# A unit's convolution two slots behind its correlation products instead of one, with five x buffers, two volume buffers and an unrolled program

## The reference

```python
def _L0_conv_ref(feature, conv_w, conv_b):
    norm = jnp.sqrt(jnp.sum(feature * feature, axis=1, keepdims=True))
    fn = feature / jnp.maximum(norm, EPS)
    fp = jnp.pad(fn, ((0, 0), (0, 0), (PAD, PAD), (PAD, PAD)))      # PAD = 2
    sims = []
    for cc in range(5):
        for r in range(5):
            sims.append(jnp.sum(fp[:, :, r:h + r, cc:w + cc] * fn, axis=1))
    x = jnp.concatenate([feature, jnp.stack(sims, axis=1)], axis=1)  # 512 + 25 channels
    out = jnp.einsum('bihw,oi->bohw', x, conv_w) + conv_b[None, :, None, None]
    return jax.nn.relu(out)

x = x + _L0_conv_ref(_gn(x), L0_conv_conv_w, L0_conv_conv_b)   # _gn: 32 groups
x = x + _L1_conv_ref(_gn(x), L1_conv_conv_w, L1_conv_conv_b)   # the same form
```

## Time and profile before

| | |
|---|---|
| median of three runs | 577.4 us |
| span of the profiled execution | 584.5 us |
| PE busy | 510.0 us (87%) |
| DVE busy | 407.1 us (70%) |
| ACT busy | 259.9 us (44%) |
| POOL busy | 137.2 us (23%) |
| DMA queue share | 35.2% of 16 engines |

### The profile page before, as it was taken

The page is one execution under the profiler, slowest core; times in us unless marked ns, Lnnn a source line. Parts: engine busy times, 40 slices in busy tenths (PEclk is TensorE's granted clock), DMA queues, the critical chain, the costliest instruction groups (busy, mean ns, idle before and its releaser), DMA issues.

```text
span 584.5 us, 8565 instructions
## 1 busy us (share of the span) xinstructions
PE 510.0 (87%) x2888; PEld 287.5 (49%) x2888; DVE 407.1 (70%) x856; ACT 259.9 (44%) x350; POOL 137.2 (23%) x87
## 2 busy tenths in 40 slices
PE   0358779998999699997999979998999989998996
PEld 0246336464645446463464635555464646454442
DVE  5879697785868487756868477785978868672322
ACT  1343364635445263643645344453636364543332
POOL 3352625031030404012040400304040312204050
PEclk9986999999999989997999979999999999999999
DMA  8753103121135612355042721347132512334313
GB/s 342 255 192 134 57 4 102 38 88 56 52 115 164 207 38 88 127 177 181 14 128 113 226 91 34 118 167 230 32 100 85 202 38 70 110 119 140 128 41 144
DMA packets 47484, 69.37 MB, mean 119 GB/s; under 512 B 3848, under 2 KB 36616, under 8 KB 47448
## 3 DMA queue, kind: packets, MB, share of 16 engines
q1 hardware_dynamic: 47448, 68.93, 35.2%
HBM read 33.21 MB, written 35.71 MB: 118 GB/s over the span
## 4 chain that ended last, share of the span: by engine, by line
PE 45%; DVE 19%; issue 19%; POOL 8%; ACT 4%; DMA 3%; DVEq 1%; SPq 0%; ACTq 0%; POOLq 0%
PE conv_ps L456 32%; PE gram_ps L481 7%; DVE xs L806 3%; PE conv_ps L463 3%; DVE stats L639 3%; POOL corr L398 2%; POOL corr L396 2%; POOL mirror L393 2%; PE turn_ps L508 2%; DVE v L692 2%; ACT act_out L608 2%; DVE vol L703 2%; DVE opnd L697 2%; ACT vol L558 1%; DVE nbr L734 1%
## 5 line engine op out<-in xcount | busy, mean ns | idle before, releaser
L456 PE MATMUL conv_ps<-opnd,wh 128*128 128x512 f16 x512 | 198.4, 387 | 0.2 <-ACT act_out L608 0.2
L456 PE MATMUL conv_ps<-opnd,wl 128*128 128x512 f16 x512 | 198.3, 387 | 0.0
L456 PE MATMUL conv_ps<-opnd,whh 128*128 128x512 f16 x512 | 197.8, 386 | 0.0
L608 ACT ACTIVATE act_out<-conv_ps,bias,wdown 128x512 f32<-128x512 f32 x128 | 97.3, 773 | 131.8 <-PE conv_ps L463 130.4
L393 POOL TENSOR_TENSOR mirror<-mirror,rn_own 25x1024 f32<-25x1024 f32 x16 | 38.3, 2396 | 378.3 <-DMA rn_own<-rows_dram 378.3
L481 PE MATMUL gram_ps<-opnd 128*128 128x256 f16 (+1 forms) x1024 | 112.5, 273 | 13.7 <-DVE opnd L697 11.7
L806 DVE TENSOR_TENSOR xs<-xs,act_out 128x512 f32<-128x512 f32 (+1 forms) x128 | 87.2, 696 | 50.7 <-ACT act_out L608 50.3
L481 PEld LDWEIGHTS gram_ps<-opnd 128*128 128x128 f16 x1024 | 99.3, 100 | 28.4 <-issue 14.2
L697 DVE SCALAR_TENSOR_TENSOR opnd<-opnd,v 128x1024 f16<-128x1024 f16 x64 | 80.8, 1266 | 11.0 <-POOL v L405 4.1
L639 DVE BATCH_NORM_STATS2 stats<-xs 128x6 f32<-128x512 f32 (+1 forms) x128 | 78.4, 680 | 12.2 <-POOL nbr L368 5.8
L456 PEld LDWEIGHTS conv_ps<-opnd,whh 128*128 128x128 f16 x512 | 50.9, 99 | 63.4 <-issue 5.0
(11 more groups left out here) (65 smaller groups left out, 221.5 us busy)
## 6 DMA issues: line engine op xcount, KB each, us to landing
xs<-in_x_dram SPq DMA_DIRECT2D x32, 512.0 KB, 4.5
band_dram<-band SPq DMA_DIRECT2D x64, 256.0 KB, 2.4
out_dram<-xs SPq DMA_DIRECT2D x32, 512.0 KB, 2.7
skew<-band_dram SPq DMA_DIRECT2D x16, 532.0 KB, 4.0
opnd<-in_L_conv_conv_w_dram SPq DMA_DIRECT2D x2, 1074.0 KB, 12.2
rows_dram<-rows SPq DMA_DIRECT2D x16, 131.6 KB
mirror<-rows_dram SPq DMA_DIRECT2D x16, 112.1 KB
rn_far<-rows_dram SPq DMA_DIRECT2D x16, 112.1 KB
```

The source lines that it names most:

```text
L456: pe.matmul(conv_ps[:, g % 4, :], w[:, l, t, m * P:(m + 1) * P], opnd[:, slot, part, t, n * HALF:(n + 1) * HALF], start=(t == 0 and w is w ...
L608: act.activation(act_out[:, g % 2, :], conv_ps[:, g % 4, :], ACT.Relu, bias=bias[:, l, m:m + 1], scale=wdown[:, l, m:m + 1]).then_inc(relu, 1)
```

## The change

The convolution of unit k-2 stands in slot k (`LAG = 2`), so a correlation volume has one slot more before it is read, and is kept in two buffers (`vol` has a third index). Units go in teams of four batches: layer 0 of batches 0 to 3, layer 1 of them, then the same for batches 4 to 7. `xs` has five buffers. The result of `correlation` is written over `rn_far`, and there is no `corr` buffer. There are no loops. The transposes stand at g = 5, and for units 1 and 2 at g = 0 of the next slot. In slot 0 four groups of `channels` of unit 0 stand already. The second layer's weights are turned in slot 4 rather than 1. POOL makes `v2` for units 0 to 3 rather than 0 and 1.

```diff
-LEAD = 2
+TEAM = 4
+LAG = 2
 RING = 4
+XRING = 5
 def unit_layer(u):
-    if u <= LEAD:
-        return 0
-    return 1 if u % 2 or u > UNITS - LEAD - 2 else 0
+    return u // TEAM % LAYERS
...
-    BACK = 64
+    BACK = 32
...
-        vol = sb("vol", [P, PIX], F16)
+        vol = sb("vol", [P, 2, PIX], F16)
...
-        V2_ON_POOL = (0, 1)
+        V2_ON_POOL = (0, 1, 2, 3)
         AFFINE_AT = lambda k0: 0 if k0 > 1 else FIRST_AT(k0)
-        NORM_AT = lambda k0: {0: 4, 1: 1}.get(k0, 2)
-        TURN_AT = lambda k0: 5 if k0 == 0 else 4
-        HOLD = 1
+        NORM_AT = lambda k0: {0: 4, 1: 4, 2: 6}.get(k0, 2)
+        TURN_LATE = (1, 2)
+        VOL_AT = lambda k0: {1: 4, 2: 7, 3: 6}.get(k0, 1)
+        def turned_in(k0, g):
+            if k0 - 1 in TURN_LATE and g == 0:
+                return k0 - 1
+            return k0 if valid(k0) and k0 not in TURN_LATE and g == 5 else None
         W_AT = 3
+        W1_SLOT = 4
...
+                if left:
+                    for t in range(KT):
+                        tile_in(u - 1, t)
                 if finished:
-                    tile_out(k, k0, i, 0)
-                    tile_in(k, k0, i, 0)
-                    tile_out(k, k0, i, 1)
-                if valid(k0):
+                    tile_out(u, 0)
+                    tile_out(u, 1)
+                if valid(k0) and k0 not in TURN_LATE:
                     rows_to_dram(k, k0 % 2)
-                if finished:
-                    tile_in(k, k0, i, 1)
...
                 pool.tensor_tensor(mir, mir, near, ALU.mult).then_inc(corr_step, 1)
-                wait(pool, vol_low, k)
-                wait(pool, vol_high, 2 * k)
-                pool.tensor_tensor(dst, own, far, ALU.mult).then_inc(corr_step, 1)
+                pool.tensor_tensor(far, own, far, ALU.mult).then_inc(corr_step, 1)
...
+                    if k0 == 0 and g == 7:
+                        pe.wait_ge(w_half, KT)
+                        pe.wait_ge(w_low, KT)
+                        for h in range(4):
+                            channels(0, 0, 0, h)
+                            if h == 2:
+                                average(2)
...
-                    if g == hold:
+                    if g == 0:
                         pe.wait_ge(vol_high, 2 * (u + 1))
                         pe.wait_ge(vol_low, u + 1)
-                        for h in range(hold):
-                            volume(l, h)
-                    if g >= hold:
-                        volume(l, g)
+                    if u > 0 or g >= 4:
+                        channels(u, slot, l, g)
+                    volume(u, l, g)
...
             def step(k, k0, i):
-                u0, u = k0 - 1, k - 1
+                u0 = u = k0 - LAG
+                if k0 == 1:
+                    deviations(2)
+                    act.wait_ge(gn_step, GN_STEPS * 3)
+                    for t in range(2):
+                        norm_tile(2, 2, 0, t)
...
-                if valid(u0):
-                    volume_high(u)
...
                 for g in range(GROUPS):
+                    if g == VOL_AT(k0) and valid(k0 - 1):
+                        volume_high(k0 - 1)
...
+                    if g == FIRST_AT(k0) and valid(k0 + 1) and k0 != 1:
+                        deviations(k0 + 1)
...
+                    v = turned_in(k0, g)
+                    if v is not None:
+                        first_rows(v)
                     if g == AFFINE_AT(k0) and valid(k0 + 1):
                         unit_affine(k, k0)
                     if g == NORM_AT(k0) and valid(k0):
                         norms(k)
                         neighbours(k)
+                    if g == min(VOL_AT(k0) + 1, GROUPS - 1) and valid(k0 - 1):
+                        volume_low(k0 - 1)
```

More of the change, by code:

```diff
@@ L154, in build @@
         bias = sb("bias", [P, LAYERS, KT], F32)
-        w_raw = [opnd[:, RING - LAYERS + l, :, :, :].rearrange("p a t n -> p (a t n)").bitcast(F32)
-                 [:, 0:KT * CI].rearrange("p (t n) -> p t n", t=KT) for l in range(LAYERS)]
+        w_raw = [a[:, 0:KT * CI].rearrange("p (t n) -> p t n", t=KT) for a in (
+            opnd[:, RING - 1, :, :, :].rearrange("p a t n -> p (a t n)").bitcast(F32),
+            xs[:, XRING - 1, :, :].rearrange("p t n -> p (t n)"))]
         conv_ps = ps("conv_ps", [P, 4, HALF], F32)
@@ L167, in build @@
         w_in = [sem(f"w_in{l}") for l in range(LAYERS)]
-        x_in = [[sem(f"x_in{q}_{t}") for t in range(KT)] for q in range(2)]
+        x_in = [[sem(f"x_in{q}_{t}") for t in range(KT)] for q in range(XRING)]
         x_out = [sem(f"x_out{t}") for t in range(KT)]
@@ L215, in ring_slot @@
         def ring_slot(b):
-            return b % RING
+            return b % XRING
         def slots(eng, step):
-            for k in range(-1, FIRST_LOOPED):
-                step(k, k, 0)
-            with eng.Fori(0, TRIPS) as i:
-                for k0 in range(FIRST_LOOPED, FIRST_LOOPED + PERIOD):
-                    step(k0 + PERIOD * i, k0, i)
-            for k in range(LAST_LOOPED + 1, UNITS + 1):
+            for k in range(-1, UNITS + LAG):
                 step(k, k, 0)
@@ L338, in step @@
                     for t in range(2, KT):
-                        tile_out(k, k0, i, t)
-                    for t in range(2, KT):
-                        tile_in(k, k0, i, t)
+                        tile_out(u, t)
             slots(sp, step)
@@ L415, in step @@
                     half_weights(0)
-                if valid(k0):
-                    correlation(k)
-                if k0 == 0:
+                if k0 == W1_SLOT:
+                    half_weights(1)
+                if valid(k0) and k0 != 1:
+                    if k0 == 2:
+                        correlation(1)
+                    correlation(k0)
+                if k0 == W1_SLOT - 1:
                     scaled_weights(1)
-                    half_weights(1)
             slots(pool, step)
@@ L458, in channels, with volume @@
                                   start=(t == 0 and w is wh), stop=False)
-            def volume(l, g):
+            def volume(u, l, g):
                 m, n = g // 2, g % 2
                 pe.matmul(conv_ps[:, g % 4, :], wvol[0:96, l, m * P:(m + 1) * P],
-                          vol[0:96, n * HALF:(n + 1) * HALF], start=False, stop=True).then_inc(conv, 1)
+                          vol[0:96, u % 2, n * HALF:(n + 1) * HALF], start=False, stop=True).then_inc(conv, 1)
             def step(k, k0, i):
@@ L545, in high_weights, with deviations @@
                                    ).then_inc(w_high, 1)
+            def deviations(u):
+                act.wait_ge(gn_step, GN_STEPS * u + 4)
+                act.activation(gstd[:, :], gvar[:, :], ACT.Sqrt).then_inc(gn_root, 1)
             def norm_tile(u, u0, i, t):
-                xt = xs[:, ring_slot(unit_batch(u0) + 2 * i), t, :]
+                xt = xs[:, ring_slot(unit_batch(u0)), t, :]
                 act.activation(opnd[:, u0 % RING, 0, t, :], xt, ACT.Identity, bias=affine[:, 0, 1, t:t + 1],
@@ L796, in step @@
                     if k0 == 0 and g == 7:
-                        for n in range(KT):
+                        for n in range(KT + 1):
                             low_weights(0, n)
-                        scale_weights(1)
-                    if k0 != 0 and g == TURN_AT(k0) and valid(k0):
-                        first_rows(k)
                     if valid(u0):
                         m, n = g // 2, g % 2
-                        xt = xs[:, ring_slot(unit_batch(u0) + 2 * i), m, n * HALF:(n + 1) * HALF]
+                        xt = xs[:, ring_slot(unit_batch(u0)), m, n * HALF:(n + 1) * HALF]
                         dve.wait_ge(relu, GROUPS * u + g + 1)
```

178 lines of the change are left out of this document (79 added, 99 removed).

## The result

| | before | after |
|---|---|---|
| median of the runs, same chip | 578.84 us (577.38 to 581.96, 4 runs) | 593.19 us (591.83 to 595.35, 4 runs) |
| ratio, 95% interval | | 1.0253 (1.0198 to 1.0307) |
| span of the profiled execution | 584.5 us | 593.6 us |
| products of slot 5 begin | 188.0 us | 187.6 us |
| slots 5 to 14 | 334.1 us | 326.3 us |

The kernel is 2.5% slower; forecast were 584 us and 1.1%. The time lies inside the range of 565 to 594, by 0.8 us, and in the case of 0.55 (slower). It lies outside the 578 to 591 of the likeliest case, and the slowdown, 14.4 us, is more than twice the forecast one. Ratios and spreads use the fast executions alone; two slow ones of the kernel before, of 582.36 and 585.75 us, are left out of them.

What follows compares the result with a forecast made beforehand. PE, busy 510 of 584.5 us, was taken as the bound, though not everywhere. Start 187, ten slots 324 and end 80 made a 591 us span, less 7.1: 584 us, 1.1% slower, range 565 to 594.

Steps and rivals of the forecast that it cites:

- the case of 0.55 (slower): Whole kernel: chance 0.55 that it is slower by more than the 0.5% a measurement can tell.
- the likeliest case: Whole kernel: slower, 578 to 591 us with 584 in the middle, through late weights and early groups; chance 0.48.
- G = S + L + 7.3: Regular slots: root starts (G) L plus 7.3 us after products start (S); L runs from DMA to POOL's first pass.
- P = L + 24.6: Regular slots: period when ACT waits for the correlation; 32.0 us with L = 7.4, 33.1 with L = 8.5.
- Rival 3: Regular slots at PE's pace, the correlation ending before group 1: ten slots 306 us, kernel time 566 us; chance 0.15.
- Ten slots: Slots 5 to 14: six of 32.0 and four of 33.1 us, 324 us against 334.1 before.
- the side step: Regular slots: PE idles about 2 us in each; such a stop costs clock, but not time.
- The end: Slot 15 to the end, with one more convolution: 80.0 us, a gain of 4.9 against 84.9.
- The start: Until slot 5's products: 187 us, between 178 without holds and 190 with full holds of DVE; 21.5 us lost.
- Rival 2: Start: POOL and DVE hardly disturb each other, slot 5 starts at 178, kernel time 575 us; chance 0.20.
- Less the 7.1 us between profile and runs: Whole kernel: 7.1 us taken off the forecast span of 591 us, giving 584 us.
- Rival 4: Ten slots: views wait behind stores, L near 9 everywhere, low clock reaches the root; 12 us more, 596 us; chance 0.17.

Runs made afterwards that it cites:

- e1: Kernel after, with the volume of unit k-1 made in group 3 instead of group 1, behind the root: 573.42 us, ratio 0.9925 to the kernel before.
- e7: Kernel after, in its own order, with correlation passes of units 4 to 15 on the first image row only: 574.82 us, ratio 0.9898.
- e10: e1 with correlation passes of units 1, 2 and 3 on the first image row only: 559.27 us, ratio 0.9653.
- e11: The program of e1 unchanged, measured again on another chip: 574.23 us, ratio 0.9909.
- e9: e10 plus three full POOL passes on otherwise unused memory behind each of the three short correlations: 572.30 us, ratio 0.9874.
- e5: The kernel before, unchanged, profiled a second time: 581.26 us, ratio 1.0025, span 578.8 us.
- e3: Kernel after, with v of units 2 and 3 made on DVE instead of POOL: 592.28 us, ratio 1.0243.

## Why the prediction came out as it did

- **Direction and mechanism: right.** PE's wait for the volume went, and ACT's wait for the correlation now holds the root and, through it, the period. The prediction has the correlation "no longer waited for by PE", but "waited for by ACT"; ACT waited for it before too (49.0 us), only not with DVE behind it. The formula G = S + L + 7.3 gives S + 15.6 for slot 10; the row says S + 15.8. P = L + 24.6 holds in all nine slots with a wait, to 0.1 us: 32.9 and 34.2 for slots 10 and 11, measured 33.0 and 34.3. e1 and e7 show from two sides that this wait is the whole difference between 30.5 and 32.6 us. Rival 3 is e1 as a kernel, with 305 us for the forecast 306.
- **Ten slots: 324 forecast, 326.3 measured, partly by luck.** Slot 5 had no wait and took 30.5 us, for 32.0 forecast. In the nine others L was 8.2 on the mean (7.28 to 9.61), for 7.84 taken. And L did not follow the stores. With stores issued behind the views (slots 7 to 10) it was 8.42, 7.55, 7.28 and 8.33; in slots 11 and 12, without any load or store of x near them, it was 9.61 and 8.85. What sets L is open.
- **Clock: the side step held, narrowly.** Stops of about 2 us "cost clock, but not time". Of the nine stops ahead of the products of slots 6 to 14, two had slow products behind them, here that of slot 8:

```profile
284.12 8.38 PE L486 MATMUL gram_ps<-opnd 128*128 128x192 f16 x64 [2.53 <-issue]
```

The granted clock was 0.80 from 284.1 to 292.6, and again after the 1.93 us at 481.24; behind the other stops, 2.53 us among them, the products took 6.72 us at 1.00. So the length of the stop alone doesn't tell. In these two slots ACT came to the volume at S + 12.0 instead of S + 10.3 and still waited there, 0.21 and 0.67 us: the low clock used up the wait and cost nothing beyond it.

- **The end: 80.0 forecast, 79.7 measured.**
- **The start: 187 forecast, 187.6 measured,** and on the way 64.1, 75.6, 107.1 and 147.1 us for 65, 78, 106 and 140 to 151. The sum is right and its parts were not. Slot 3's 106 came from `affine` at 93.5 and 12.6 us for `v` and `opnd` passes that exclude each other. In e10, where the correlation passes are short, POOL's first `v` starts at 90.70 and the products at 102.46, 11.8 us later, so this price was about right. But `affine` was ready 2 us before the forecast, and the correlation's passes, which the prediction put behind these products, already began at 100.17 and added some 4 us (15.6 us in e11 for the 11.8). Two errors cancelled. The bound was wrong as well: with short passes slot 5 starts at 171 and not at 178. Holds of DVE are worth most of the 13 us of e9. I had counted holds one by one over the operations of one chain; e9's nine idle passes of 2.1 us make 19 us, of which two thirds reach the end. Rival 2 ("POOL and DVE hardly disturb each other") had it wrong: the operations beside the passes were held.
- **The step that failed: "Less the 7.1 us between profile and runs".** It was taken as a constant between two ways of measuring, from one profiled execution and three runs. A run is 1.7 to 1.8 us longer than its own span in each of the twelve profiled executions that have both numbers; e5's span of 578.8 us lies among the runs. The span was right within 2.6 us (591 against 593.6); with the gap that all later runs show, 591 + 1.7 = 592.7 us would have been forecast, for 593.19 measured. The same long execution was the base of the difference. Against e5 the kernel after loses 0.0 at the start, gains 5.5 in the ten slots (10.1 forecast) and loses 20.3 in the end, where the extra convolution of 22.5 was forecast less 4.9 and came less 2.2. That is +14.8 us of span, and the runs show 593.19 - 578.84 = 14.4.
- **Rival 4** (596 us) names nearly the right time by the wrong way: L was not near 9 everywhere and didn't follow the stores, and the low clock did not delay the root.

The Trainium skill (SBUF — State Buffer, Who interferes with whom) has such a hold last for the whole instruction, and lets `tensor_scalar` take part in a two-port mode even though it has one input in SBUF. The traces agree: `v`, a `tensor_scalar`, took 2.85 us beside a pass (e3) and 0.81 without one.

## What to carry to other kernels

Where a queue holds two unrelated items, put the one that closes a loop across iterations first: here the volume had a slot to spare and the root had none, and their order was worth 21 us of 594. Freeing one engine from a ring leaves the ring in place if another engine still carries it: before and after, ACT made the volume ahead of the root, and only e1 broke that. Before a difference between a profile and the runs is used as a constant, ask for a second profiled execution, or compare spans with spans. And when work is handed to POOL beside a busy DVE, count POOL's passes against DVE's time wherever DVE has no idle time (here the start, 13 us), and at nothing where it has (here the regular slots, 18 us of holds and no change of the period).

## What was not expected of the hardware

POOL and DVE alternated when both had such operations queued: 3.31 + 2.46 + 3.22 us of POOL beside 2.84 + 3.03 + 2.84 us of DVE in 9 us of time. Passes on unrelated memory hold DVE too (10.7 us for nine). In the kernel after a DVE operation of 128x4, 0.16 us long elsewhere, was held for most of a pass of 2.35 us:

```profile
388.85 2.33 DVE L655 TENSOR_TENSOR gtmp<-mv 128x4 f32<-128x4 f32 x1
```

It stays open why the kernel before spreads over 7 us from run to run on one chip while e1 does not. Its volume waits differ little between the two profiled executions (20.9 and 19.6 us), and 3.0 of their 5.7 us lie in the end, where the granted clock was 0.96 and 1.00.
